# Low-rank weight tiles: loads moved to SyncE's queue, eight ahead, with six output buffers

## The chip, the cores and the metric

One core of one Trainium2 chip runs the kernel. The metric is the device time of one execution in microseconds (us). Engines are named as in the profile: PE is TensorE, DVE is VectorE, ACT is ScalarE, POOL is GpSimd, SP is SyncE, which here only issues transfers. SPq and ACTq are the instruction streams that issue transfers; a transfer's issue takes the issuing engine's time, its data lands later.

## The reference

Two attention-like and two feed-forward layers on x of 1024 rows by 512, each as `x = x + layernorm(layer(layernorm(x)))`. What matters here is the first layer and the weights of the last:

```
# layer 1: causal attention, 32 query heads of 16, 8 key/value groups, 4 heads each
q = x @ Wq ; kv = x @ Wkv ; softmax(q k^T / 4, causal) @ v ; @ Wo + bo
# layer 4: feed-forward whose three matrices have a low-rank part (rank 16)
out = x @ w.T + (x @ a.T) @ b.T          # gate, up: 1376 x 512; down: 512 x 1376
```

## The kernel before

The kernel folds the low-rank part of layer 4 into its weights: `w + b a` is computed once, tile by tile, and stored to DRAM (`lora_d`, `lorad_d`), from where it is read much later. There are 38 such tiles, `lora_jobs`: 0 to 10 of gate and 11 to 21 of up, 128 x 512 in float32 (the last of each has 96 rows), and 22 to 37 of down, 128 x 344. They are computed in the kernel's opening, in the gaps of the attention's projections and first scores.

One tile k takes five steps on four engines. PE multiplies `lora_bt` by `lora_at` (`lora_job`, L1078) into a PSUM bank; ACT copies it into an output buffer (`lora_take`, L899); POOL adds the weight tile that was loaded from DRAM (`pool_lora`, L1020); ACT issues the store (`lora_store`, L888) and, right behind it, the load of weight tile k + 4 into the buffer just read (`lora_load`, L882). ACT issues the store of tile k only after it took tile k + 2. Both rings have 4 buffers of 2 KiB per partition, so `lora_take` of tile k waits until the store of tile k - 4 has landed:

```
act.wait_ge(lora_ready, k + 1)
if k >= 4:
    act.wait_ge(lora_stored[k % 4], 16 * (k // 4))
```

The two operands: `lora_bt` is made by a DMA transpose (L398), `lora_at` by six copies from SBUF to SBUF (L400), all issued by SP once DVE has split the factors into bf16 pieces (`lora_split`).

Around this, the opening goes so. PE makes five projections of 16 float32 matmuls each (L1702): j = 0 the keys, j = 1 to 4 the queries, j = 1 holding those of groups 0 and 1. After each, ACT copies the PSUM banks to bf16 (L1669), DVE makes two further pieces (L1627 to L1631), SP stores the three (L1531) to `kp_d` or `qp_d`, and SP loads them back with another layout: the keys into `kt6` (L1535, six loads), a group's queries into `qt6` (`load_q`, L1253, six loads). SP's order is written by hand: stores of j = 0, loads of the keys, stores of j = 1, load of group 0's queries and a wait until it landed, stores of j = 2, 3, 4, three small loads (`sp_early`), load of group 1's queries, three hops.

With projection 4 PE begins the early scores (L1453): 80 score blocks, 48 of group 0 and 32 of group 1, of which eight lie in projection 4. DVE reduces each to row maxima (`row_max`, L1365 and L1369). When group 0 is through, `max_pieces` raises `m3_ready`, and SP sends the maxima by three hops (a DMA transpose L1260, a store L1263, a load L1266) into group 0's queries (`m_loaded`). Low-rank products 0 to 3, 4 to 7 and 8 to 11 are put between the matmuls of projections 2, 3 and 4 (`LORA_IN`), the other 26 (`LORA_LATE`) evenly between the 72 early scores that are left; PE waits with product k until product k - 4 was taken.

The group loop starts when all 38 tiles are taken (PE), the maxima of group 0 have landed, and all 38 stores have landed (ACT, `all_lora_stored`, since its output buffer overlaps theirs). Its eight groups follow one another, and then the feed-forward and the other layers.

Of the kernel before, what the change touches and what calls it, by code (L numbers as in the profile page):

```python
# [6 lines left out]
T, D = 1024, 512  # L7
NT, ND = T // P, D // P
# [70 lines left out]
def build(nc, x_in, Wq, Wkv, Wo, bo, gate_t, up_t, down_t, gate_s, up_s, down_s,  # L79
          gate_w, up_w, down_w, gate_a, gate_b, up_a, up_b, down_a, down_b, dft, power, inverse, out):  # L80
    with ExitStack() as ctx:
# [3 lines left out]
        def sem(name):  # L85
            return ctx.enter_context(nc.semaphore(name))
# [179 lines left out]
        lora_clear, lora_split, lora_stacked = sem("lora_clear"), sem("lora_split"), sem("lora_stacked")  # L266
        lora_w_loaded = [sem(f"lora_w_loaded{i}") for i in range(4)]
        lora_in, lora_ready, lora_taken = sem("lora_in"), sem("lora_ready"), sem("lora_taken")
        lora_stored = [sem(f"lora_stored{i}") for i in range(4)]
        prep_loaded = [sem(f"prep_loaded{b}") for b in range(4)]  # L270
# [55 lines left out]
        lora_bres = room(71.25, [NB, RANK])  # L326
        lora_out = room(176, [4, D])
        lora_w = room(152, [4, D])
        lora_jobs = [(m, n, 0) for m in range(2) for n in range(N1)] + [(2, n, j) for n in range(ND) for j in range(4)]
# [65 lines left out]
        def sp_lora_stack(sp):  # L395

            sp.wait_ge(lora_split, 1)
            sp.dma_start_transpose(lora_bt[:, :, :], lora_bs.rearrange("p n c -> p (n c)")).then_inc(lora_stacked, 16)  # L398
            for t, (_, piece) in enumerate(TERMS):
                sp.dma_start(lora_at[RANK * t:RANK * (t + 1), :], lora_ap[0:RANK, piece, :]).then_inc(lora_stacked, 16)  # L400
# [474 lines left out]
        def lora_bank(k):  # L875

            return 6 + k % 2 if k < LORA_LATE[0] else 4 + (k - LORA_LATE[0]) % 4

        def lora_load(act, k):

            src = lora_tile((gate_w, up_w, down_w), *lora_jobs[k])
            act.dma_start(lora_w[0:src.shape[0], k % 4, 0:src.shape[1]], src).then_inc(lora_w_loaded[k % 4], 16)  # L882

        def lora_store(act, k):

            act.wait_ge(lora_added, k + 1)
            dst = lora_tile((lora_d[0], lora_d[1], lorad_d), *lora_jobs[k])
            act.dma_start(dst, lora_out[0:dst.shape[0], k % 4, 0:dst.shape[1]]).then_inc(lora_stored[k % 4], 16)  # L888
            if k + 4 < len(lora_jobs):
                lora_load(act, k + 4)  # L890

        def lora_take(act, k):

            m, n, _ = lora_jobs[k]
            h, w = (height(m, n), D) if m < 2 else (P, FF1 // 4)
            act.wait_ge(lora_ready, k + 1)
            if k >= 4:
                act.wait_ge(lora_stored[k % 4], 16 * (k // 4))
            nc.scalar.copy(lora_out[0:h, k % 4, 0:w], ps[0:h, lora_bank(k), 0:w]).then_inc(lora_taken, 1)  # L899
            if k >= 2:  # L900
                lora_store(act, k - 2)


        LORA_IN = {j: range(4 * (j - 2), 4 * (j - 1)) for j in range(2, 1 + ND)}
        LORA_LATE = range(LORA_IN[ND][-1] + 1, len(lora_jobs))

        def all_lora_stored(engine):

            for k in range(4):
                engine.wait_ge(lora_stored[k], 16 * len(lora_jobs[k::4]))  # L910

# [102 lines left out]
        def pool_lora(pool):  # L1014

            for k, (m, n, j) in enumerate(lora_jobs):
                h, w = (height(m, n), D) if m < 2 else (P, FF1 // 4)
                pool.wait_ge(lora_taken, k + 1)
                pool.wait_ge(lora_w_loaded[k % 4], 16 * (k // 4 + 1))
                nc.gpsimd.tensor_tensor(lora_out[0:h, k % 4, 0:w], lora_out[0:h, k % 4, 0:w], lora_w[0:h, k % 4, 0:w],  # L1020
                                        ALU.add).then_inc(lora_added, 1)
# [492 lines left out]
        def _(sp):  # L1514
# [8 lines left out]
            sp.wait_ge(lora_clear, 1)  # L1523
            sp_lora(sp)
            sp_lora_stack(sp)

            for j in range(1 + ND):
# [9 lines left out]
                if j == 1:  # L1537
                    sp.wait_ge(pieces_stored[1], 48)
                    load_q(sp, 0)
                    sp.wait_ge(qt_loaded, 16 * len(TERMS))  # L1540
            sp.wait_ge(pieces_stored[0], 48 * 3)
            sp.wait_ge(pieces_stored[1], 48 * 2)
            sp_early(sp)
            load_q(sp, 1)
            for hop in range(3):
                maxima_hop(sp, 0, hop)

# [105 lines left out]
        def _(act):  # L1653
# [7 lines left out]
            for j in range(1 + ND):  # L1661
# [8 lines left out]
                if j == 0:  # L1670
                    act.wait_ge(v_psum, 1)
                    nc.scalar.copy(vall[:, :, :, :].rearrange("p t g d -> p (t g d)"),
                                   ps[:, 6:8, :].rearrange("p b n -> p (b n)")).then_inc(v_ready, 1)
                    for k in range(4):
                        lora_load(act, k)
            for k in LORA_LATE:
# [10 lines left out]
        def _(pe):  # L1687
# [36 lines left out]
            for j in range(1, 1 + ND):  # L1724
                if j >= 2:
                    pe.wait_ge(res_ready, j - 1)
                if j == 2:
                    pe.wait_ge(v_ready, 1)
                    pe.wait_ge(lora_stacked, 16 * 7)
# [89 lines left out]
```

## Time and profile before

| | |
|---|---|
| median of 3 runs | 921.38 us (920.71 to 922.01) |
| the profiled execution | 920.06 us, of it the span 918.0 us |
| busy in the span | PE 749.4 us, DVE 670.1, PEld 408.7, ACT 363.9, POOL 291.7 |
| PE clock granted, mean | 0.908 |
| DMA packets | 133360 on queue q1, 10816 on q10, 240 on q0 |
| low-rank stores issued by ACT to `lora_d` | 20 of 256 KB, median 4.5 us to landing |

Times are from the start of the span. A row of the timeline shows start, duration, engine, line, operation and, in brackets, the idle time before it and what ended it. Busy shares over the whole span say little of the opening, which is the first 150 us; it is read by stages. q1 is SP's queue and q10 is ACT's.

### The profile page before, as it was taken

How to read it: one execution, taken by the hardware profiler on the slowest of the kernel's cores; microseconds unless marked ns; L12 is line 12 of the kernel's file. 1: busy time of each engine (PE TensorE's matmuls, PEld its weight loads, DVE VectorE, ACT ScalarE, POOL GpSimd, SP SyncE). 2: the span in 40 equal slices, each digit the busy share in tenths (PEclk: the TensorE clock that was granted, in tenths of full speed). 3: DMA queues.
4: the chain of work that ended last, by engine and by line, in shares of the span. 5: the costliest groups of instructions: out<-in, count | busy, mean ns of one | idle time of the engine just before them, and what ended most of it. 6: DMA issues, size and time to landing. Idle time of an engine off the chain costs nothing. (4 is left out here: it accounts for less than half of the span.)

```text
span 918.0 us, 16061 instructions
## 1 busy us (share of the span) xinstructions
PE 749.4 (82%) x5081; PEld 408.7 (45%) x5102; DVE 670.1 (73%) x1781; ACT 363.9 (40%) x699; POOL 291.7 (32%) x348
## 2 busy tenths in 40 slices
PE   1967666879898898988869998696969999788694
PEld 1623221223222222222327676474747777566472
DVE  7523875766776767797489999896998999955713
ACT  1212224545565545677104444343433534323121
POOL 4024443102021120232104555345524335224131
PEclk9988656989899999998979999898989999899798
DMA  9499889772131312644451375613645221110100
GB/s 265 74 177 341 237 245 225 150 165 60 29 60 28 49 39 39 154 121 135 107 159 25 98 141 109 187 24 86 81 98 94 43 35 25 24 46 1 46 24 24
DMA packets 144477, 93.38 MB, mean 102 GB/s; under 512 B 111832, under 2 KB 123224, under 8 KB 144200
## 3 DMA queue, kind: packets, MB, share of 16 engines
q1 hardware_dynamic: 133360, 70.19, 34.4%
q10 hardware_dynamic: 10816, 16.91, 5.9%
q0 software_dynamic: 240, 5.51, 2.9%
q8 instruction: 33, 0.54, 0.3%
q14 instruction: 28, 0.23, 0.1%
HBM read 48.47 MB, written 29.04 MB: 84 GB/s over the span
## 5 line engine op out<-in xcount | busy, mean ns | idle before, releaser
L1205 PE MATMUL ps<-arena 128*128 128x256 f16 (+1 forms) x1952 | 238.2, 279 | 23.9 <-DMA arena<-arena 23.9
L1205 PEld LDWEIGHTS ps<-arena 128*128 128x128 f16 (+1 forms) x1952 | 196.4, 101 | 68.5 <-DMA arena<-arena 16.9
L1432 ACT ACTIVATE arena<-ps 128x1024 f32<-128x1024 f32 (+7 forms) x256 | 163.6, 651 | 123.4 <-PE ps L1462 118.8
L1453 PE MATMUL ps<-arena 96*128 (+4 forms) x384 | 137.0, 382 | 39.9 <-DVE mx L1369 15.5
L1365 DVE CUSTOM_DVE_ANT_0 arena<-ps,arena 128x256 bf16<-128x256 f32 (+3 forms) x256 | 122.0, 488 | 57.2 <-PE ps L1453 49.4
L1057 POOL TENSOR_TENSOR arena<-arena 128x256 f32<-128x256 f32 (+1 forms) x100 | 80.3, 803 | 258.3 <-ACT arena L948 257.6
L1227 PE MATMUL ps<-arena 128*128 128x512 f16 (+2 forms) x467 | 119.6, 385 | 32.6 <-POOL arena L1063 31.2
L1462 PE MATMUL ps<-arena 99*128 (+4 forms) x384 | 128.6, 352 | 4.6 <-ACT arena L1432 4.2
L1340 POOL TENSOR_SCALAR_AFFINE_SELECT arena<-arena 128x512 f32<-128x512 f32 x64 | 42.2, 659 | 230.4 <-ACT arena L1432 230.2
L1369 DVE TENSOR_REDUCE mx<-ps 128x1 f32<-128x512 f32 x128 | 88.2, 689 | 32.1 <-PE ps L1453 31.2
L1453 PEld LDWEIGHTS ps<-arena 96*128 (+1 forms) x384 | 39.3, 102 | 150.0 <-issue 81.0
L1485 PE MATMUL ps<-arena 128*32 128x256 f32 (+1 forms) x1280 | 100.7, 388 | 3.1 <-POOL arena L1340 2.3
L1227 PEld LDWEIGHTS ps<-arena 128*128 128x128 f16 (+1 forms) x488 | 46.1, 99 | 74.0 <-POOL arena L1063 36.6
L1063 POOL TENSOR_TENSOR arena<-arena 128x256 f16<-128x256 f32 (+1 forms) x100 | 77.6, 776 | 0.0
L1020 POOL TENSOR_TENSOR arena<-arena 128x512 f32<-128x512 f32 (+2 forms) x38 | 43.5, 1150 | 87.3 <-ACT arena L899 50.9
L947 ACT ACTIVATE arena<-ps,gs 128x256 f32<-128x256 f32 (+1 forms) x44 | 20.8, 473 | 122.4 <-PE ps L1205 122.4
L947 ACT ACTIVATE arena<-ps,sc 128x256 f32<-128x256 f32 x56 | 26.5, 474 | 85.3 <-PE ps L1205 85.3
L1462 PEld LDWEIGHTS ps<-arena 99*128 (+1 forms) x384 | 36.6, 100 | 41.2 <-issue 16.5
L1485 PEld LDWEIGHTS ps<-arena 128*32 128x32 f32 x1280 | 26.0, 110 | 53.4 <-issue 43.1
L1702 PE MATMUL ps<-arena 128*128 128x512 f32 x80 | 42.3, 660 | 6.8 <-DMA arena<-arena 6.0
L899 ACT COPY arena<-ps 128x512 f32<-128x512 f32 (+2 forms) x38 | 20.0, 526 | 66.0 <-DMA lora_d<-arena 28.1
L1183 PE MATMUL ps<-arena 128*128 128x256 f16 (+2 forms) x336 | 40.4, 280 | 7.0 <-DMA arena<-arena 6.3
(163 smaller groups left out, 851.9 us busy)
## 6 DMA issues: line engine op xcount, KB each, us to landing
arena<-qp_d SPq DMA_DIRECT2D x48, 128.0 KB, 4.1
lora_d<-arena ACTq DMA_DIRECT2D x20, 256.0 KB, 4.5
arena<-lora_d SPq DMA_DIRECT2D x10, 512.0 KB, 5.1
w1n_d<-arena SPq DMA_DIRECT2D x10, 512.0 KB, 3.6
arena<-rec_d SPq DMA_DIRECT2D x32, 128.0 KB, 2.6
qp_d<-arena SPq DMA_DIRECT2D x12, 256.0 KB, 4.9
w1dn_d<-arena SPq DMA_DIRECT2D x4, 704.0 KB, 3.8
arena<-in_L_ffn_down_w_dram ACTq DMA_DIRECT2D x16, 172.0 KB, 3.6
```

The source lines that it names most:

```text
L947: nc.scalar.activation(sg[0:h, b, :], ps[0:h, b, 0:CH], ACT.Silu, scale=gate[0:h, ht:ht + 1]).then_inc(sg_ready, 1)
L1020: nc.gpsimd.tensor_tensor(lora_out[0:h, k % 4, 0:w], lora_out[0:h, k % 4, 0:w], lora_w[0:h, k % 4, 0:w], ALU.add).then_inc(lora_added, 1)
L1057: nc.gpsimd.tensor_tensor(hs[0:h, b, :], sg[0:h, b, :], u_sb[0:h, b, :], ALU.mult).then_inc(hs_ready, 1)
L1063: nc.gpsimd.tensor_tensor(hid[0:h, 1, b, :], hs[0:h, b, :], hid[0:h, 0, b, :], ALU.subtract).then_inc(hid_ready, 1)
L1205: last = nc.tensor.matmul(ps[0:h, b, CH * o:CH * (o + 1)], w(t[0])[:, kt, ht * P:ht * P + h], xt[:, c, t[1], kt, :], start=(kt, t) == (0, ...
L1227: last = nc.tensor.matmul(ps[:, y_bank(k, i), :], hid[0:h, t[0], b, i * P:(i + 1) * P], down[0:h, ht, :], start=ht == 0 and t == terms[0], ...
L1365: nc.vector.tensor_tensor_reduce(out=junk[:, h, 0:w], in0=s_bank(g, u)[:, 0:w], in1=strip[:, D - w:D], scale=1.0, scalar=3.0 * NEG, op0=AL ...
L1369: nc.vector.reduce_max(mx[:, h, qt:qt + 1], s_bank(g, u)[:, 0:w], mybir.AxisListType.X).then_inc(s_taken, 1)
L1432: nc.scalar.activation(probs[:, kt % 2, h, kt * P:T], st_bank(h).rearrange("p b n -> p (b n)")[:, kt * P:T], ACT.Exp, scale=HD ** -0.5).th ...
L1453: nc.tensor.matmul(s_bank(g, u)[:, 0:k1 - k0], qt6[0:QROWS, g % RING, h, qt * P:(qt + 1) * P], kt6[0:QROWS, g, k0:k1], start=True, stop=Tr ...
L1462: last = nc.tensor.matmul(st_bank(h)[:, b, q0 - b * 512:512], kt6[0:QROWS + MROWS, g, kt * P:(kt + 1) * P], qt6[0:QROWS + MROWS, g % RING, ...
L1485: last = nc.tensor.matmul(o_bank[32 * h:32 * h + 32, b, q0 - b * 512:q1 - b * 512], vcur[:, kt, :], probs[:, kt % 2, h, q0:q1], start=kt = ...
```

## The change

The loads of the weight tiles go from ACT to SP, in a ring of 8 buffers: the first eight at the start, once the buffers' bytes are free (`xnt_psum`), 8 to 11 behind the piece stores of j = 3, 12 to 23 behind those of j = 4, and the rest between and behind the maxima's hops; load k waits until tile k - 8 was added. The output ring gets 6 buffers. The DMA transpose of `lora_bt` goes from SP to ACT. The products start one projection later: 0 to 3 in j = 3, 4 to 7 in j = 4, 30 late ones; with them moves PE's wait for the operands. The load of group 1's queries goes ahead of the stores of j = 2, and `sp_early` behind all loads.

```diff
@@ -264,9 +264,9 @@
         w0_loaded = [sem(f"w0_loaded{i}") for i in range(3)]
         lora_added = sem("lora_added")
         lora_clear, lora_split, lora_stacked = sem("lora_clear"), sem("lora_split"), sem("lora_stacked")
-        lora_w_loaded = [sem(f"lora_w_loaded{i}") for i in range(4)]
+        lora_w_loaded = [sem(f"lora_w_loaded{i}") for i in range(8)]
         lora_in, lora_ready, lora_taken = sem("lora_in"), sem("lora_ready"), sem("lora_taken")
-        lora_stored = [sem(f"lora_stored{i}") for i in range(4)]
+        lora_stored = [sem(f"lora_stored{i}") for i in range(6)]
         prep_loaded = [sem(f"prep_loaded{b}") for b in range(4)]
         prep_done = sem("prep_done")
         prep_stored = [sem(f"prep_stored{b}") for b in range(4)]
@@ -324,8 +324,10 @@
         lora_bt = room(63, [NB, P], BF16)
         lora_b = room(69.5, [NB, RANK])
         lora_bres = room(71.25, [NB, RANK])
-        lora_out = room(176, [4, D])
-        lora_w = room(152, [4, D])
+        LORA_DEEP = 8
+        LORA_OUT = 6
+        lora_out = room(176, [LORA_OUT, D])
+        lora_w = room(152, [LORA_DEEP, D])
         lora_jobs = [(m, n, 0) for m in range(2) for n in range(N1)] + [(2, n, j) for n in range(ND) for j in range(4)]
 
 
@@ -395,7 +397,6 @@
         def sp_lora_stack(sp):
 
             sp.wait_ge(lora_split, 1)
-            sp.dma_start_transpose(lora_bt[:, :, :], lora_bs.rearrange("p n c -> p (n c)")).then_inc(lora_stacked, 16)
             for t, (_, piece) in enumerate(TERMS):
                 sp.dma_start(lora_at[RANK * t:RANK * (t + 1), :], lora_ap[0:RANK, piece, :]).then_inc(lora_stacked, 16)
 
@@ -876,38 +877,44 @@
 
             return 6 + k % 2 if k < LORA_LATE[0] else 4 + (k - LORA_LATE[0]) % 4
 
-        def lora_load(act, k):
-
-            src = lora_tile((gate_w, up_w, down_w), *lora_jobs[k])
-            act.dma_start(lora_w[0:src.shape[0], k % 4, 0:src.shape[1]], src).then_inc(lora_w_loaded[k % 4], 16)
+        def lora_transpose(act):
+
+            act.wait_ge(lora_split, 1)
+            act.dma_start_transpose(lora_bt[:, :, :], lora_bs.rearrange("p n c -> p (n c)")).then_inc(lora_stacked, 16)
+
+        def lora_loads(sp, jobs):
+
+            for k in jobs:
+                if k >= LORA_DEEP:
+                    sp.wait_ge(lora_added, k - LORA_DEEP + 1)
+                src = lora_tile((gate_w, up_w, down_w), *lora_jobs[k])
+                sp.dma_start(lora_w[0:src.shape[0], k % LORA_DEEP, 0:src.shape[1]], src).then_inc(lora_w_loaded[k % LORA_DEEP], 16)
 
         def lora_store(act, k):
 
             act.wait_ge(lora_added, k + 1)
             dst = lora_tile((lora_d[0], lora_d[1], lorad_d), *lora_jobs[k])
-            act.dma_start(dst, lora_out[0:dst.shape[0], k % 4, 0:dst.shape[1]]).then_inc(lora_stored[k % 4], 16)
-            if k + 4 < len(lora_jobs):
-                lora_load(act, k + 4)
+            act.dma_start(dst, lora_out[0:dst.shape[0], k % LORA_OUT, 0:dst.shape[1]]).then_inc(lora_stored[k % LORA_OUT], 16)
 
         def lora_take(act, k):
 
             m, n, _ = lora_jobs[k]
             h, w = (height(m, n), D) if m < 2 else (P, FF1 // 4)
             act.wait_ge(lora_ready, k + 1)
-            if k >= 4:
-                act.wait_ge(lora_stored[k % 4], 16 * (k // 4))
-            nc.scalar.copy(lora_out[0:h, k % 4, 0:w], ps[0:h, lora_bank(k), 0:w]).then_inc(lora_taken, 1)
+            if k >= LORA_OUT:
+                act.wait_ge(lora_stored[k % LORA_OUT], 16 * (k // LORA_OUT))
+            nc.scalar.copy(lora_out[0:h, k % LORA_OUT, 0:w], ps[0:h, lora_bank(k), 0:w]).then_inc(lora_taken, 1)
             if k >= 2:
                 lora_store(act, k - 2)
 
 
-        LORA_IN = {j: range(4 * (j - 2), 4 * (j - 1)) for j in range(2, 1 + ND)}
+        LORA_IN = {j: range(4 * (j - 3), 4 * (j - 2)) for j in range(3, 1 + ND)}
         LORA_LATE = range(LORA_IN[ND][-1] + 1, len(lora_jobs))
 
         def all_lora_stored(engine):
 
-            for k in range(4):
-                engine.wait_ge(lora_stored[k], 16 * len(lora_jobs[k::4]))
+            for k in range(LORA_OUT):
+                engine.wait_ge(lora_stored[k], 16 * len(lora_jobs[k::LORA_OUT]))
 
 
         def down_read(engine, n):
@@ -1016,8 +1023,8 @@
             for k, (m, n, j) in enumerate(lora_jobs):
                 h, w = (height(m, n), D) if m < 2 else (P, FF1 // 4)
                 pool.wait_ge(lora_taken, k + 1)
-                pool.wait_ge(lora_w_loaded[k % 4], 16 * (k // 4 + 1))
-                nc.gpsimd.tensor_tensor(lora_out[0:h, k % 4, 0:w], lora_out[0:h, k % 4, 0:w], lora_w[0:h, k % 4, 0:w],
+                pool.wait_ge(lora_w_loaded[k % LORA_DEEP], 16 * (k // LORA_DEEP + 1))
+                nc.gpsimd.tensor_tensor(lora_out[0:h, k % LORA_OUT, 0:w], lora_out[0:h, k % LORA_OUT, 0:w], lora_w[0:h, k % LORA_DEEP, 0:w],
                                         ALU.add).then_inc(lora_added, 1)
 
         def pool_rest(pool):
@@ -1522,6 +1529,8 @@
                              Wo[half, :].rearrange("(c p) n -> p c n", p=P // 2)).then_inc(wo_loaded, 16)
             sp.wait_ge(lora_clear, 1)
             sp_lora(sp)
+            sp.wait_ge(xnt_psum, NT)
+            lora_loads(sp, range(LORA_DEEP))
             sp_lora_stack(sp)
 
             for j in range(1 + ND):
@@ -1538,12 +1547,19 @@
                     sp.wait_ge(pieces_stored[1], 48)
                     load_q(sp, 0)
                     sp.wait_ge(qt_loaded, 16 * len(TERMS))
+                    load_q(sp, 1)
+                if j == 3:
+                    lora_loads(sp, range(8, 12))
             sp.wait_ge(pieces_stored[0], 48 * 3)
             sp.wait_ge(pieces_stored[1], 48 * 2)
+            lora_loads(sp, range(12, 24))
+            maxima_hop(sp, 0, 0)
+            lora_loads(sp, range(24, 28))
+            maxima_hop(sp, 0, 1)
+            lora_loads(sp, range(28, 32))
+            maxima_hop(sp, 0, 2)
+            lora_loads(sp, range(32, len(lora_jobs)))
             sp_early(sp)
-            load_q(sp, 1)
-            for hop in range(3):
-                maxima_hop(sp, 0, hop)
 
             sp_group(sp, 0, 0, 0, 0)
             sp_tables(sp)
@@ -1671,8 +1687,7 @@
                     act.wait_ge(v_psum, 1)
                     nc.scalar.copy(vall[:, :, :, :].rearrange("p t g d -> p (t g d)"),
                                    ps[:, 6:8, :].rearrange("p b n -> p (b n)")).then_inc(v_ready, 1)
-                    for k in range(4):
-                        lora_load(act, k)
+                    lora_transpose(act)
             for k in LORA_LATE:
                 lora_take(act, k)
             for k in range(len(lora_jobs) - 2, len(lora_jobs)):
@@ -1724,7 +1739,7 @@
             for j in range(1, 1 + ND):
                 if j >= 2:
                     pe.wait_ge(res_ready, j - 1)
-                if j == 2:
+                if j == 3:
                     pe.wait_ge(v_ready, 1)
                     pe.wait_ge(lora_stacked, 16 * 7)
                 if j == ND:
```

The instruction order of SP in the opening, before. The rows from the copies of the low-rank operand to the last piece stores (L400 the copies, L1531 stores, L1535 the keys' loads, L1253 a group's queries):

```order
L398 DMA_TRANSPOSE arena<-arena 128x26x128
L400 DMA arena<-arena 16x2400 x6
L1531 DMA kp_d<-arena 128x1024 x3
L1535 DMA arena<-kp_d 16x8x1024 x6
L1531 DMA qp_d<-arena 128x1024 x3
L1253 DMA arena<-qp_d 16x4x1024 x6
L1531 DMA qp_d<-arena 128x1024 x9
```

The same place of SP's stream in the changed kernel (L891 is a weight tile's load, L401 the copies, L1540 stores, L1544 the keys' loads, L1260 the queries'):

```order
L891 DMA arena<-in_L_ffn_gate_w_dram 128x512 x8
L401 DMA arena<-arena 16x2400 x6
L1540 DMA kp_d<-arena 128x1024 x3
L1544 DMA arena<-kp_d 16x8x1024 x6
L1540 DMA qp_d<-arena 128x1024 x3
L1260 DMA arena<-qp_d 16x4x1024 x12
L1540 DMA qp_d<-arena 128x1024 x6
L891 DMA arena<-in_L_ffn_gate_w_dram 128x512 x2
L891 DMA arena<-in_L_ffn_gate_w_dram 96x512
L891 DMA arena<-in_L_ffn_up_w_dram 128x512
L1540 DMA qp_d<-arena 128x1024 x3
```

The transpose is gone from SP, eight loads stand ahead of the copies, and twelve query loads stand together, six of them ahead of the stores of j = 2. Further on in SP's stream, around the hops of the maxima (in this kernel L1267, L1270 and L1273), the changed kernel has:

```order
L891 DMA arena<-in_L_ffn_up_w_dram 96x512
L891 DMA arena<-in_L_ffn_down_w_dram 128x344 x2
L1267 DMA_TRANSPOSE mt<-m 128x128
L891 DMA arena<-in_L_ffn_down_w_dram 128x344 x4
L1270 DMA mt_d<-mt 128x128
L891 DMA arena<-in_L_ffn_down_w_dram 128x344 x4
L1273 DMA arena<-mt_d 3x4096
L891 DMA arena<-in_L_ffn_down_w_dram 128x344 x6
L377 DMA sc<-in_L_ffn_gate_s_dram 128x14x1
L378 DMA sc<-in_L_ffn_up_s_dram 128x14x1
L379 DMA row_b<-in_L_attn_bo_dram 128x512
```

Before, the three hops stood next to each other with nothing between. On PE, the start of the projections before (L1692 transposes, L1702 projections, L1720 the values, L1078 low-rank products):

```order
L1692 MATMUL ps<-ident,arena 128x128 x32
L1702 MATMUL ps<-arena 128x512 x8
L1720 MATMUL ps<-arena 128x128 x32
L1702 MATMUL ps<-arena 128x512 x9
L1078 MATMUL ps<-arena 128x512
L1702 MATMUL ps<-arena 128x512
```

and in the changed kernel (L1707, L1717, L1735 and L1085 are the same four):

```order
L1707 MATMUL ps<-ident,arena 128x128 x32
L1717 MATMUL ps<-arena 128x512 x8
L1735 MATMUL ps<-arena 128x128 x32
L1717 MATMUL ps<-arena 128x512 x17
L1085 MATMUL ps<-arena 128x512
L1717 MATMUL ps<-arena 128x512
```

Sixteen projection matmuls go through where eight did, before the first product and its wait.

## Rows read from the trace of the kernel before

**Rows 1.** Stages of the opening: length, busy (count) per engine, PEclk, DMA share, GB/s.

```profile
27.00:40.00 13.00, 13.00 (x71) 9.17 (x72) 10.13 (x11) 1.01 (x1) 0.00 (x0) 1.00 0.09 16
...
41.00:54.10 13.10, 7.08 (x18) 2.91 (x18) 5.35 (x6) 2.03 (x2) 0.00 (x0) 0.94 1.03 214
54.10:72.80 18.70, 14.56 (x31) 5.96 (x31) 3.14 (x3) 3.94 (x6) 5.35 (x5) 0.86 0.97 197
72.80:82.60 9.80, 8.01 (x13) 3.15 (x12) 0.92 (x1) 3.35 (x5) 4.71 (x4) 0.65 1.03 287
82.60:96.40 13.80, 9.47 (x31) 3.82 (x31) 10.67 (x19) 3.56 (x6) 6.50 (x5) 1.00 0.77 278
96.40:110.00 13.60, 11.99 (x36) 3.86 (x36) 12.75 (x52) 3.34 (x7) 8.38 (x7) 0.64 0.95 284
110.00:123.80 13.80, 7.02 (x19) 1.95 (x18) 8.00 (x24) 3.05 (x6) 5.83 (x6) 0.50 0.88 256
123.80:142.70 18.90, 11.85 (x38) 4.05 (x38) 14.04 (x56) 4.45 (x10) 9.07 (x10) 0.50 0.87 231
```

**Rows 2.** Timeline, 40 to 55 us: the low-rank operands and projection 2.

```profile
40.18 3.98 SPq L398 DMA_TRANSPOSE arena<-arena  x1
...
41.26 3.60 ACTq L882 DMA_DIRECT2D arena<-in_L_ffn_gate_w_dram  x4
...
44.21 4.01 SPq L400 DMA_DIRECT2D arena<-arena  x6
...
48.27 3.12 SPq L1531 DMA_DIRECT2D kp_d<-arena  x3
...
54.12 2.04 PE L1702 MATMUL ps<-arena 128*128 128x512 f32 x2 [6.04 <-DMA arena<-arena]
```

**Rows 3.** Timeline, 58 to 93 us: query stores, loads, first scores.

```profile
58.30 1.42 SPq L1531 DMA_DIRECT2D qp_d<-arena  x3
...
61.05 4.46 PE L1702 MATMUL ps<-arena 128*128 128x512 f32 x10
...
72.83 2.78 SPq L1253 DMA_DIRECT2D arena<-qp_d  x6
...
74.29 7.17 PE L1702 MATMUL ps<-arena 128*128 128x512 f32 x10
...
82.64 0.39 PE L1453 MATMUL ps<-arena 96*128 96x512 bf16 x1 [0.96 <-DMA arena<-qp_d]
...
92.22 1.01 ACT L1669 CAST arena<-ps 128x1024 bf16<-128x1024 f32 x1 [3.51 <-PE ps L1702]
```

**Rows 4.** Query loads of two later groups (L1253, 185 to 240 us): time to landing.

```profile
DMA to landing us min/median/max: 2.9/3.7/4.7
```

**Rows 5.** Waits, 96.4 to 150.2 us: total, times, longest.

```profile
ACT arena L899 <- DMA lora_d<-arena: 18.6, 9, 4.1
ACT arena L899 <- DMA lorad_d<-arena: 14.2, 10, 3.7
```

**Rows 6.** Groups of POOL, 96.4 to 148.2 us: busy, mean ns, idle before.

```profile
L1020 POOL TENSOR_TENSOR arena<-arena 128x344 f32<-128x344 f32 x16 | 14.5, 907 | 12.5 <-DMA arena<-in_L_ffn_down_w_dram 9.6 <-ACT arena L899 2.7
L1020 POOL TENSOR_TENSOR arena<-arena 128x512 f32<-128x512 f32 x9 | 11.7, 1307 | 16.5 <-DMA arena<-in_L_ffn_up_w_dram 10.6 <-ACT arena L899 5.9
```

**Rows 7.** Low-rank stores (L888, 96 to 150 us): time to landing.

```profile
DMA to landing us min/median/max: 1.8/3.2/8.6
```

**Rows 8.** Weight tiles' loads (L882, 96 to 150 us): time to landing.

```profile
DMA to landing us min/median/max: 2.6/4.0/9.3
```

**Rows 9.** The first hop's transpose (L1260, 100 to 180 us): time to landing.

```profile
DMA to landing us min/median/max: 3.8/5.9/8.1
```

**Rows 10.** Timeline, 123 to 151 us: first hop, end of the opening.

```profile
123.85 1.15 SPq L1260 DMA_TRANSPOSE mt<-m  x1
...
146.97 0.61 PE L1453 MATMUL ps<-arena 96*128 96x512 bf16 x1 [4.90 <-ACT arena L899]
...
150.14 1.94 ACT L1432 ACTIVATE arena<-ps 128x1024 f32<-128x1024 f32 x2 [3.22 <-DMA lorad_d<-arena]
```

## The prediction

> **What bounds it now.** I read the opening by stages first, since the change touches nothing behind it. In the stages [rows 1] the reader is to see that until 96.4 us no compute engine is full, while the DMA share is about 1.0 from 41 to 82.6 us; and that it was 0.09 from 27 to 40 us. Then the timeline [rows 2, 3] tells which transfer is waited for. Projection 2 starts at 54.12 after 6.04 us of waiting for a DMA: the copies of the low-rank operand, issued from 44.21, behind a transpose that held SP from 40.18. The same SP then stores the keys (48.27), and a strict chain follows, each link waiting for the landing of the one before: keys stored, keys loaded, queries of j = 1 stored (58.30), queries of group 0 loaded (72.83), first score (82.64). So the front is a chain of transfers, not PE.
>
> From 96.4 us on DVE could set the pace: it is busy 12.75 of 13.6 us, then 8.00 of 13.8 (to the first hop at 123.85 [rows 10]), then 14.04 of 18.9 [rows 1]. The 10 to 11 us that it lacks behind 110 us come from the low-rank ring: ACT waits 18.6 + 14.2 us for landed stores before it may take a tile [rows 5], PE waits for ACT and the scores stand behind PE's products. The end is the ring's too: PE starts the loop at 146.97 after 4.90 us of waiting for ACT, and the first exponential, at 150.14, waits for the last store [rows 10]. That start, 150.14, is the event I move. What follows is a loop whose transfers and casts are issued relative to it, so I carry a shift through to the end at full value; an earlier start has the same cold PE clock (0.50 [rows 1]) as now.
>
> **Part by part.**
>
> *Eight loads at 28 us, transpose to ACT.* The eight loads are 2 MB in a stretch where the DMA engines did 16 GB/s [rows 1], and the four that ACT issued at 41.26 [rows 2] are gone from the crowded one. At the issue times of that row (3.60 us for 4) eight take about 7 us, over by 35, before SP's next wait ends at 40.18. ACT issues the transpose at 41.3, free until its copy of 48.1, so it costs ACT nothing. SP's copies go out at 40.18 instead of 44.21 and the keys' stores at 44.2 instead of 48.27: minus 4.0. Bounds: minus 2 if transpose, copies and stores now share engines and land later, minus 4.1 by issue. PE's wait of 6.04 us leaves the front of projection 2; I count nothing for it, because PE then only comes sooner to the wait for group 0's queries.
>
> *Keys to group 0's queries.* 72.83 minus 58.30 is 14.5 us, mostly the keys' slow loads; four low-rank stores still fall beside them. I leave this link unchanged (bounds minus 2, plus 2). The next link took 9.8 us (72.83 to 82.64) beside the stores and loads of some four low-rank tiles on ACT's queue (POOL's four adds in that stage [rows 1]). Now no low-rank load stands there. Six issues take 2.78 us [rows 3] and a quiet landing 3.7 (at most 4.7) [rows 4]: 6.5 us, minus 3.3. Upper bound 9.8 as before. First score: 82.6 - 4.0 - 3.3 = 75.3.
>
> *Projection 4.* PE now is at its wait from about 64 us (projections 2 and 3 from 48 us on, 7.1 us each at the 4.46 us for ten matmuls of [rows 3], and four products with ACT's takes) and stands 11 us, so its clock will have fallen. The price is in two rows of equal work: ten projection matmuls took 4.46 us at 61.05 and 7.17 at 74.29 [rows 3]: 2.7 us. Against it stand 1.5 us, since DVE has finished the pieces of j = 3 by then and PE needn't wait for it as it did now and then before. The projection took 9.6 us (82.64 to 92.22) [rows 3]; it will take 10.8 and end at 86.1. Group 1's queries and the stores of j = 2, which ACT's copy needs, are issued from 75.3 to 80 and should land by 85. Shift at the end of the pieces (96.4 before): minus 6.1.
>
> *Late scores up to the first hop.* DVE's work there is 12.75 + 8.00, 20.8 us [rows 1], in 27.4 us. With six buffers the ring is no more the brake: take k + 6 needs store k, issued behind take k + 2, so four tiles turn in about 0.6 + 0.3 + 3.2 + 0.6, 4.7 us [rows 7], 1.2 us a tile; by the longer landing of 8.6 it would be 2.5, as slow as now. POOL needs 1.31 us a tile of 512 and 0.91 of 344 [rows 6], which is now the ring's pace. Tile 12's load stands behind the landing of the last piece stores and costs POOL a gap of 2 to 3 us, which the ten tiles of slack in banks and buffers mostly absorb. I add 1.7 us of stall: 22.5 us instead of 27.4, minus 4.9. Bounds: minus 6.6 (none), 0 (landings as long as their longest). First hop at 112.8.
>
> *From the first hop to the loop.* SP issues loads 24 to 27 only when the maxima are ready, 28 to 31 only when the transpose has landed, 32 to 37 only when the store behind it has. This is the wait that the change adds, and behind it stand POOL, ACT, PE. With the transpose at 5.9 us [rows 9], a store at 3.2 and a tile load at 4.0 [rows 8], and about 1.5 us of issues between, loads 32 on land 14.6 us after the hop; six more adds are 5.4 us, the last store 3.2: 23.2 us. The scores alone want DVE 14.04 us, so they don't decide. Before it was 150.14 - 123.85, 26.3 us: minus 3.1. With the shortest landings (3.8, 1.8, 2.6, the last store 1.8) it is 16.9 us, minus 9.4; with the longest (8.1, 8.6, 9.3, the last store as above) 36.1, plus 9.8.
>
> *Nothing for the rest.* `sp_early` and group 2's queries now come at 127 to 132 us, ahead of the loop's start; their cover is its first part. Were it gone, each would cost its landing, 4 us.
>
> Sum: -4.0 - 3.3 + 1.2 (together minus 6.1), -4.9, -3.1: **minus 14.1 us**. First exponential at 136.0; the profiled execution 920.06 - 14.1 = 906.0, and 1.3 us more against the median shown, 921.38: **907.3 us**.
>
> **Weighed against the skill.** The late stages must move their 11.8 MB (rates by lengths in [rows 1]) in some 41 us instead of 46: 288 GB/s, just what the stages from 72.8 and 96.4 us reached, so there is room, but not much. The Trainium skill, "DMA: Bandwidth & Descriptors", section "Issuing engines are not separate DMA queues", says that transfers issued from SP and ACT run on the same 16 engines, so that spreading them saves issue time only. By it alone the ring's part of the gain would have to come from the buffers, or not at all, which is the first rival's time.
>
> **Rivals.**
> - *The DMA engines are the limit.* For it: share 0.87 to 0.95 behind 96.4 us [rows 1]. Against it: the bytes, and 0.09 ahead of 40 us, where 2 MB now go. The late stages then keep their 46 us and the front brings 6.1: 915.3.
> - *All landings short.* The front as forecast, 6.1, and the lower bounds of the two late stages, 6.6 and 9.4: minus 22.1, 899.3.
> - *The change does nothing:* if the loop start were held by something else. POOL's adds total only 26 us in 52 [rows 6], and nothing else waits at 146.97. 921.
> - *Slower: loads trapped between the hops.* One mechanism: the last 14 tiles wait for two landings of a three-link chain and then for their own. If the landings there are the longest seen, 36.1 us instead of 26.3, the loss is 9.8 there, less 6.1 in the front, and crowded engines that let landings grow so leave the scores' stage where it was: 925.1. It decides from 32.4 us on (26.3 + 6.1); with the scores' gain, from 37.3. The skill's page of the same title, section "Queues, rings and completion order", says that an engine takes from each queue in turn; by it the hops, now behind tile loads in SP's own queue, come later, and the stores, alone in ACT's, sooner. No row here shows the two apart.
>
> **Chances and range.** Forecast (902 to 911) 0.60; DMA limit 0.20; short landings 0.10; nothing 0.04; slower 0.06. What a measurement can tell from no change is 0.2%, 1.8 us. Faster 0.90, same 0.04, slower 0.06. The range takes in the forecast, most of the first rival and the near part of the second: 902 to 915.5.
>
> **What would show it.** In the new profile: eight gate loads by 35 us; no PE wait at projection 2, but one of about 11 us in projection 4; first score near 75, first hop near 113, with DVE over 90% busy between 90 and 113; POOL waiting for down tiles at two places behind the hop; first exponential near 136; from there on a copy of the old trace. It is wrong if the first score comes at 80 or later (the queries' landing), if ACT still waits over 20 us for stores, or if the time from the first hop to the loop grows beyond 28 us.

## The result, and the profile after

The changed kernel is slower: 925.31 us median (918.56 to 933.49, 20 runs) against 922.07 (916.25 to 930.42, 20 runs) before, ratio 1.0049, interval 1.0028 to 1.0071. The forecast was 907.3, faster. Its profiled execution took 928.51 us, span 926.4; before's 920.06, span 918.0.

The opening of the changed kernel by stages (columns as in [rows 1]; the second to last is the DMA share):

```profile
27.00:40.00 13.00, 13.00 (x76) 9.41 (x76) 9.61 (x11) 1.01 (x1) 0.00 (x0) 1.00 0.57 178
...
92.60:117.60 25.00, 18.86 (x57) 6.30 (x57) 22.46 (x74) 9.16 (x17) 18.80 (x16) 0.64 0.93 325
117.60:134.80 17.20, 12.18 (x39) 4.22 (x39) 13.90 (x56) 4.97 (x12) 10.74 (x13) 0.50 0.92 257
...
134.80:160.10 25.30, 4.02 (x9) 1.04 (x9) 3.42 (x7) 0.00 (x0) 2.61 (x4) 0.50 0.94 219
```

The eight loads fill the gap ahead of 40 us. Until 134.8 us things go as forecast, less well but in the same direction: DVE is busy 22.46 of 25.0 us up to the first hop. Then comes a stage that has no counterpart before: 25 us in which ACT does nothing and PE 4 us of work, with the DMA share at 0.94. The timeline of the changed kernel, with the events that answer to those of [rows 2], [rows 3] and [rows 10]:

```profile
40.71 7.11 SPq L401 DMA_DIRECT2D arena<-arena  x6
40.71 5.21 ACTq L883 DMA_TRANSPOSE arena<-arena  x1
...
47.86 2.59 SPq L1540 DMA_DIRECT2D kp_d<-arena  x3
...
70.65 10.36 SPq L1260 DMA_DIRECT2D arena<-qp_d  x12
...
78.38 0.61 PE L1460 MATMUL ps<-arena 96*128 96x512 bf16 x1 [8.01 <-DMA arena<-qp_d]
...
117.58 1.22 SPq L1267 DMA_TRANSPOSE mt<-m  x1
...
134.76 2.27 ACTq L897 DMA_DIRECT2D lorad_d<-arena  x3
134.85 0.61 PE L1460 MATMUL ps<-arena 96*128 96x512 bf16 x1 [3.17 <-ACT arena L906]
...
136.40 0.52 POOL L1607 DMA_DIRECT2D w0u_d<-in_L_ffn_up_t_dram  x1
136.91 0.50 POOL L1608 DMA_DIRECT2D w0d_d<-in_L_ffn_down_t_dram  x1
...
160.15 1.94 ACT L1439 ACTIVATE arena<-ps 128x1024 f32<-128x1024 f32 x2 [25.35 <-DMA lorad_d<-arena]
```

First score 4.3 us earlier than before (78.38 against 82.64), first hop 6.3 (117.58 against 123.85), PE's loop start 12.1 (134.85 against 146.97). Then ACT waits 25.35 us for the last stores, where it waited 3.22 [rows 10], and its first exponential is 10.0 us later than before. What stands beside those stores are the two casts that POOL issues right behind its last add (`up_t` and `down_t` to 16-bit copies in DRAM, each 1792 KB). The DMA view of 130 to 165 us, with packets, MB and share of 16 engines, and the issues with their median time to landing:

```profile
q0 software_dynamic: 160, 3.67, 48.7%
...
w0u_d<-in_L_ffn_up_t_dram POOLq DMA_DIRECT2D x1, 1792.0 KB, 14.4
w0d_d<-in_L_ffn_down_t_dram POOLq DMA_DIRECT2D x1, 1792.0 KB, 22.8
lorad_d<-arena ACTq DMA_DIRECT2D x7, 172.0 KB, 5.8
```

The landing of the last five stores (L897, 133 us on), against a longest of 8.6 before [rows 7]:

```profile
DMA to landing us min/median/max: 5.2/6.5/23.6
```

The packet records of the trace show the mechanism. The two casts travel in 128 packets of 28,672 bytes, 2.13 us each; a store's row is a packet of 1376 bytes, 0.07 us. From the records, the starts of packets in us from the span's start:

```
kernel, execution     first cast packet   last cast packet   last store packet   store packets behind the first cast packet
before                149.77              167.71             149.76              0
before, once more     148.61              166.60             148.65              3
changed               140.22              157.53             159.99              249
changed, once more    138.53              156.04             158.32              200
```

From 142.2 to 157.5 us 111 cast packets began and 120 store packets: about one small packet goes for each long one. So 249 small packets, 0.07 us of an engine's time each, last until the casts are through. In the kernel before, the last store packet began 7 ns ahead of the first cast packet; in its second profile three began behind it. By the Trainium skill, "DMA: Bandwidth & Descriptors", section "Queues, rings and completion order", each engine takes from the queues in turn, a packet at a time; the trace agrees, with 111 packets of 2.13 us beside 120 of 0.07. The forecast cited that section for the hops, and not for this.

### The profile page after: what moved, and what is told of

Read it like the earlier page. It is cut to its first block and busy times, and to the rows that moved or that the text cites. A ratio compares the mean times of both kernels' runs of the same rounds, so it can differ in the third digit from the quotient of the medians.

```text
span 926.4 us, 16081 instructions
## 1 busy us (share of the span) xinstructions
PE 749.2 (81%) x5102; PEld 407.6 (44%) x5102; DVE 674.2 (73%) x1781; ACT 363.5 (39%) x699; POOL 290.8 (31%) x348
## 5 line engine op out<-in xcount | busy, mean ns | idle before, releaser
L1234 PE MATMUL ps<-arena 128*128 128x512 f16 (+2 forms) x488 | 124.5, 386 | 29.2 <-POOL arena L1070 29.1
L954 ACT ACTIVATE arena<-ps,gs 128x256 f32<-128x256 f32 (+1 forms) x44 | 20.8, 473 | 122.7 <-PE ps L1212 122.7
L1717 PE MATMUL ps<-arena 128*128 128x512 f32 x80 | 38.8, 620 | 6.7 <-DMA arena<-kp_d 5.8
L963 ACT CAST arena<-arena 128x256 f16<-128x256 f32 (+1 forms) x100 | 40.3, 403 | 1.8 <-POOL arena L1064 1.8
```

The source lines that it names most:

```text
L954: nc.scalar.activation(sg[0:h, b, :], ps[0:h, b, 0:CH], ACT.Silu, scale=gate[0:h, ht:ht + 1]).then_inc(sg_ready, 1)
L1234: last = nc.tensor.matmul(ps[:, y_bank(k, i), :], hid[0:h, t[0], b, i * P:(i + 1) * P], down[0:h, ht, :], start=ht == 0 and t == terms[0], ...
```

## The experiments

Ten edited kernels ran, and the two kernels once more. Ratios are to the kernel before on the same chip, with their interval.

**e1_casts_wait.**

```diff
             pool_lora(pool)
+            all_lora_stored(pool)
             pool.dma_start(w16_d[1], up_t).then_inc(w0_cast[1], 16)
```

> The changed kernel, with GpSimd waiting for the landing of all low-rank stores before it issues the two casts. Theory (the last stores are starved behind the casts' 28,672-byte packets, 2.1 us each): the first exponential, at 160.15 us in the changed kernel, comes at about 141, 4 to 6 us behind the last store's issue; about 907 to 910 us, ratio to before near 0.985. Rival (the stores are held by the 4-byte packets and query loads of SyncE's own queue, or by the stores themselves): the exponential stays near 160 and the time near 925.

Measured: 911.87 us, ratio 0.9914 (0.9884 to 0.9944). The last store packet is at 142.93, the first cast packet at 145.30, and the timeline has

```profile
143.27 1.94 ACT L1439 ACTIVATE arena<-ps 128x1024 f32<-128x1024 f32 x2 [8.02 <-DMA lorad_d<-arena]
```

The casts made the stall: without them beside the stores the exponential comes 17 us sooner. It is 2 us later than expected, and ACT's wait is still 8.02 us. SP's small loads and query loads are issued in the same moment as the last stores, which here land up to 6.9 us after their issue; in f1 below, where the small loads are gone from this place and the queries are earlier, it is at most 4.0.

**e2_act_late_wait.**

```diff
-            all_lora_stored(act)
-            for_groups(act, act_group)
+            act_group(act, 0, 0)
+            all_lora_stored(act)
+            ...
```

> The changed kernel, with ScalarE's wait for the landed stores moved behind its group 0; the casts stay where they are. Theory (everything queued is starved while the casts run): the first exponential comes right behind the first scores, near 136.5, but TensorE then waits for group 2's queries, whose load has a landing of up to 19 us, until 150 or so; about 910 to 914 us. Rival (only ScalarE's wait matters): no such second wait, about 903 us.

Measured: 914.8 us, ratio 0.9923 (0.9885 to 0.9962). The exponentials start at 136.54, and the stall comes back at the next thing that was queued, group 2's queries, issued from 133.3 with a landing of up to 22.7 us:

```profile
158.47 0.61 PE L1460 MATMUL ps<-arena 96*128 96x512 bf16 x1 [10.78 <-DMA arena<-qp_d]
```

So it isn't ACT's wait alone: a load on SP's queue is held as the stores on ACT's are. The rival is out. PE's wait ends at 158.5, later than the 150 expected.

**e3_small_loads_first.**

```diff
+            sp_early(sp)
             lora_loads(sp, range(12, 24))
...
             lora_loads(sp, range(32, len(lora_jobs)))
-            sp_early(sp)
```

> The changed kernel, with the three small loads (two scale vectors in 4-byte pieces, one bias row) ahead of tile load 12 instead of behind the last tile load. Theory with the small loads as what makes the last stores late for the casts: few or no store packets are left when the first cast packet starts, first exponential at 139 to 142, about 908 us, perhaps not in every execution. If they don't matter: 925 us, and still some 249 store packets behind the first cast packet.

Measured: 909.27 us, ratio 0.9897 (0.9851 to 0.9943). 3 store packets were behind the first cast packet (142.58 against 142.54), and

```profile
139.86 0.61 PE L1460 MATMUL ps<-arena 96*128 96x512 bf16 x1 [5.28 <-ACT arena L906]
...
143.02 1.94 ACT L1439 ACTIVATE arena<-ps 128x1024 f32<-128x1024 f32 x2 [3.21 <-DMA lorad_d<-arena]
```

With the casts left where they are the race is won again, but not because the last stores end much sooner: their last packet begins at 142.58 here and at 142.93 in e1. What changed is its distance from the last add, 1.8 us here (the add ends at 140.79), 6.3 in e1 (136.65); POOL issues the casts right behind that add. The price is that the adds end 4.3 us later than in the changed kernel (136.46) and the loop starts 5 us later on PE, since the small loads now stand ahead of the tile loads. So two 7 KB loads in 4-byte pieces and a bias row, moved behind the tile loads at no cost by the forecast, made the last stores late for the casts. Whether by their own packets or by the query loads that they push beside the last stores is not separated: here, and in f1, both are out of the way.

**e4_before_casts_wait.** The same line as in e1, in the kernel before.

> The kernel before, with GpSimd waiting for all stores before the casts. In its profiled execution the last store packet ended 7 ns ahead of the first cast packet, so nothing was starved. Theory: same within 0.3%, or a little faster and with less spread, if other executions lose that race. Rival (the later casts cost something further on): slower by up to 2 us.

Measured: 921.96 us, ratio 1.002 (0.9983 to 1.0057): no difference that the interval of some 0.4% either way can tell. Nothing shows that before loses to the casts, or that later casts cost anything.

**c1_before_casts_early.** Both casts of the kernel before, issued four adds sooner:

```diff
             for k, (m, n, j) in enumerate(lora_jobs):
+                if k == len(lora_jobs) - 4:
+                    pool.dma_start(w16_d[1], up_t).then_inc(w0_cast[1], 16)
+                    pool.dma_start(w16_d[2], down_t).then_inc(w0_cast[2], 16)
...
             pool_lora(pool)
-            pool.dma_start(w16_d[1], up_t).then_inc(w0_cast[1], 16)
-            pool.dma_start(w16_d[2], down_t).then_inc(w0_cast[2], 16)
```

> The kernel before, with GpSimd issuing the two casts four adds earlier (behind the add of tile 33, not 37), so that they start some 6 us sooner and meet the last loads and stores. Theory (whatever is queued when the casts start is starved until they end, some 18 us later): first exponential at 160 to 166 us instead of 150, about 932 to 936 us, ratio 1.012 to 1.016. Rival (the stall in the changed kernel came from something the change added on SyncE's queue): 922 us, no slower.

Measured: 934.09 us, ratio 1.0117 (1.0073 to 1.0161). 890 store packets stood behind the first cast packet (143.88). From 145.9 to 161.2 us, with no query load beside them, 111 cast packets began and 112 store packets. And

```profile
165.29 0.61 PE L1456 MATMUL ps<-arena 96*128 96x512 bf16 x1 [23.78 <-ACT arena L899]
```

The stall can be made in the kernel before, with nothing of the change in it. The first exponential, at 168.17, is later than expected and 18.0 us later than before; the span is only 14.6 longer (932.6). A part of a late start is given back further on, which the forecast had excluded.

**f1_all_apart.** The edits of e1 and e2, and:

```diff
             lora_loads(sp, range(32, len(lora_jobs)))
-            sp_early(sp)
 
             sp_group(sp, 0, 0, 0, 0)
+            sp_early(sp)
             sp_tables(sp)
```

> The changed kernel with three edits: the casts wait for all stores, ScalarE waits for them behind its group 0 only, and the three small loads go behind group 1's hops, ahead of the tables. Nothing that the loop's start needs is then behind the casts or the 4-byte packets. Theory: loop start on TensorE at 134 to 135, first exponential at 136 to 137, no wait for group 2's queries, ratio 0.983 to 0.986 (about 905 to 907 us where before has 920), which is the size forecast for the change. If the opening's gain does not carry through: no better than e1 and e3 (0.990).

Measured: 915.09 us, ratio 0.9918 (0.9883 to 0.9952); the expectation failed. The exponentials start at 139.4, earlier than in e1 or e3, but the span is 920.5 in this execution, 781 us behind that start where before has 768 (918.0 - 150.14). This profiled execution was the slowest of the ten (922.56), so some 7 of these 13 us are its own and not the kernel's. The waits of 160 to 225 us name a place for the rest:

```profile
PE ps L1460 <- DMA arena<-qp_d: 12.6, 1, 12.6
```

It is group 1, where PE waits for group 3's queries. SP issues those behind group 1's hops, the gate weights' transpose, (here) the small loads, the tables and the up weights' transpose. In e1, whose exponentials start 3.9 us later, it is 5.8 us. The kernel before has the same wait, in rows that the forecast did not look at. Its waits and SP's timeline:

```profile
PE ps L1453 <- DMA arena<-qp_d: 5.1, 1, 5.1
```

```profile
162.38 4.78 SPq L1260 DMA_TRANSPOSE mt<-m  x1
170.45 0.36 SPq L1263 DMA_DIRECT2D mt_d<-mt  x1
171.94 0.27 SPq L1266 DMA_DIRECT2D arena<-mt_d  x1
172.67 8.31 SPq L411 DMA_TRANSPOSE arena<-w0g_d  x1
...
184.12 8.23 SPq L411 DMA_TRANSPOSE arena<-w0u_d  x1
192.90 4.06 SPq L1253 DMA_DIRECT2D arena<-qp_d  x6
```

The hop at 162.38 needs 8 us until 170.45; the last cast packet ends at 169.7. In the changed kernel the stall lets the casts end first:

```profile
172.81 1.11 SPq L1267 DMA_TRANSPOSE mt<-m  x1
175.07 0.37 SPq L1270 DMA_DIRECT2D mt_d<-mt  x1
```

That hop takes 2.3 us, and the wait for the queries is gone.

**h0_before_w0u_later.** This tests the reading on the kernel before:

```diff
             all_lora_stored(sp)
-            sp_weights0(sp, 1)
-            with sp.Fori(1, ND + 1) as g:
+            sp_group(sp, 1, 1, 0, 1)
+            with sp.Fori(2, ND + 1) as g:
```

> The kernel before, with SyncE's DMA transpose of the up weights (8 us of issue) moved from ahead of group 3's query load to behind group 1's other transfers. In before's group 1 TensorE waits 5.1 us for those queries, which in the changed kernel it doesn't. Theory (that wait is what the stalled start pays back in the changed kernel): group 1 takes 38 to 39 us instead of 42.9 between its first exponentials, ratio 0.994 to 0.997. Rival (group 1's length has another cause): 42 us or more, ratio 1.0.

Measured: 920.22 us, ratio 0.9962 (0.9931 to 0.9993). No DMA wait is left in group 1, and it takes 38.5 us where before's, the second row, takes 42.9 (stages as above):

```profile
189.80:228.30 38.50, 33.90 (x257) 10.73 (x256) 27.39 (x87) 21.37 (x34) 7.63 (x10) 0.96 0.41 72
```

```profile
185.30:228.20 42.90, 35.11 (x257) 11.17 (x256) 27.55 (x87) 21.38 (x34) 7.63 (x10) 0.90 0.47 105
```

Of these 4.4 us 1.2 are PE's busy time, at a granted clock of 0.96 against 0.90, and 3.2 its idle time. By the ratio the edit is worth 0.4%, 3.5 us, as expected. The span, 916.8, shows little of it, because in this execution the opening ran later (first exponential at 154.48, for a reason not looked into).

**u1_four_buffers.** e1 with `LORA_OUT = 4`.

> e1_casts_wait with four output buffers instead of six. If the output ring set the pace of the late scores (a step of the forecast): ScalarE waits for landed stores again for 20 us or more, first exponential 5 to 8 us later than in e1 (148 to 151), ratio 0.996 to 1.0. If the loads eight ahead did it: as e1, 0.991.

Measured: 918.69 us, ratio 0.996 (0.9938 to 0.9982). First exponential at 151.41, 8.1 us later than in e1. Its waits of 88 to 150 us:

```profile
ACT arena L906 <- DMA lora_d<-arena: 20.1, 14, 4.3
ACT arena L906 <- DMA lorad_d<-arena: 16.6, 9, 4.0
```

These are 36.7 us, like the 32.8 of [rows 5]; in e1 they are 9.0. The six buffers are what opened the late stretch.

**u2_products_from_2.** e1 with `LORA_IN` and PE's wait as before, at projection 2.

> e1_casts_wait with the products from projection 2 on, as before. If the later start matters: TensorE waits at projection 2 for the operands, the queries' stores meet more traffic, first score 1 to 3 us later than 78. If it doesn't (the chain of transfers sets the first score): first score within 1 us, and four tiles fewer in the late stretch; time within 0.2% of e1.

Measured: 917.43 us, ratio 0.9968 (0.9933 to 1.0003). First score at 79.08, about as in e1. But the first exponential is at 147.9, 4.6 us later than in e1, for a reason that neither side had named:

```profile
POOL arena L1027 <- DMA arena<-in_L_ffn_gate_w_dram: 17.5, 1, 17.5
```

Twelve products are in flight before projection 4 is done, but tile 8's load stands in SP's order behind the piece stores of j = 3. The later start of the products fits the place of the loads; in the front it saves nothing (the first score is at 79.06 in e1).

**h1_best.** e1's and e3's edits, and h0's.

> The changed kernel with the casts behind all stores, the three small loads ahead of tile load 12, and the up weights' transpose behind group 1. First exponential at 141 to 144 us, no wait for group 3's queries, group 1 at 38 to 39 us; ratio 0.984 to 0.988. If the two repairs don't add up, 0.990 as e3.

Measured: 908.98 us, ratio 0.9861 (0.9825 to 0.9896), faster than both kernels. First exponential at 143.29, no DMA wait in group 1. Its interval overlaps e3's (0.9851 to 0.9943), so the ratios alone don't show that h0's edit adds to e3's.

**after_again** and **before_again.** Both kernels once more, for a second profile.

> The changed kernel once more, for its profile alone. If the stall at the casts is in every execution: first exponential at 158 to 162 us again, with over 100 store packets behind the first cast packet, and no DMA wait in group 1. If it is a matter of luck: 139 to 145.

> The kernel before once more, for its profile alone. Its profiled execution won the race of the last store against the first cast by 7 ns. If that is typical: first exponential at 149 to 151 us. If other executions lose it: up to 168.

Measured: changed 925.9 us (span 923.8), before 919.63 (span 917.6). The first exponentials are at 158.48 and 149.00, and the changed kernel has

```profile
ACT arena L1439 <- DMA lorad_d<-arena: 24.9, 1, 24.9
```

so the stall is in both of its profiled executions, and in neither of before's.

## Why the prediction was wrong

**The step that failed** is "six more adds are 5.4 us, the last store 3.2: 23.2 us", in the part from the first hop to the loop. The adds were right: POOL's last one ended at 136.46, 18.9 us behind the hop where the sum has 20.0, and POOL issued the casts there. The last store took 23.6 us and not 3.2, and the stretch from hop to first exponential 42.6 us (160.15 - 117.58) instead of 23.2. The landing was priced from stores that had no cast beside them. With the casts held back, in e1, it is at most 6.9 us: the casts made 16.7 of the 20.4 us that were missed, and what SP issues in that moment probably most of the rest (in f1, without it, at most 4.0). That POOL issues two casts right behind its last add was in the source and in before's timeline (at 147.93 us), and the forecast never asked what the last stores would share the engines with. e1 and c1 show the cause from both sides, e2 that it holds SP's queue as well as ACT's. Two of the forecast's own signs of being wrong came true here: ACT waited over 20 us for stores, and the last stretch grew beyond 28 us. Added up against before, the three parts brought -3.8, -2.4 and +16.3 us, where -6.1, -4.9 and -3.1 were forecast.

**Nothing for `sp_early`** was wrong too, and it is the change's own part in the stall. The forecast asked who waits for these loads, and not whom they delay. In the changed kernel the small loads and group 2's queries are issued from 127.8 to 136.6 us, when the last stores are; e3 shows that with the loads elsewhere only 3 packets are behind the cast, at the price of later adds.

**The front** was forecast at minus 6.1 us and brought 3.8 (the last pieces end at 92.6 against 96.4). The term of 4.0 for the keys' stores came out as 0.4: the six copies, issued while the transpose ran on ACT, took 7.11 us of issue instead of 4.01 [rows 2], so that the term fell short even of its lower bound, 2. It is so in all nine profiles that have the transpose on ACT (6.1 to 7.3 us, against 3.8 to 4.0 in the five that have it on SP), but since no run leaves the transpose out, it is not shown to be the cause. The keys and the stores of j = 1 gained 1.8 (47.86 to 70.65 against 48.27 to 72.83), and group 0's queries 2.1 instead of 3.3.

**The late scores** took 25.0 us up to the first hop instead of 22.5 (27.4 before): half the forecast gain. The step on the ring was right: in u1 four buffers cost 8.1 us, 3.0 of them ahead of the first hop. DVE stood 2.5 us, not 1.7; the larger error is in its work, 22.46 us where the sum has 20.8. Two small operations on the maxima grew, here in the kernel before, then in the changed one:

```profile
122.46 0.41 DVE L1377 TENSOR_TENSOR mx<-mx 128x16 f32<-128x16 f32 x1
122.90 0.18 DVE L1382 TENSOR_SCALAR m<-mx 128x32 bf16<-128x32 f32 x1
```

```profile
111.34 5.43 POOL L1027 TENSOR_TENSOR arena<-arena 128x512 f32<-128x512 f32 x5
114.24 1.70 DVE L1384 TENSOR_TENSOR mx<-mx 128x16 f32<-128x16 f32 x1
115.98 0.83 DVE L1389 TENSOR_SCALAR m<-mx 128x32 bf16<-128x32 f32 x1
116.85 0.19 DVE L1390 SCALAR_TENSOR_TENSOR mr<-mx,m 128x32 f32<-128x32 f32 x1
```

They lie beside adds of POOL that follow one another without a gap until 116.77, and the next operation is quick again. Six more profiles with such adds beside them show the same (e1 with 1.95 and 0.84 us, for one). In u2 POOL's adds pause from 121.14 to 127.10 us, and the same two, at 121.97, take 0.17 and 0.18. So DVE's times were taken from a stage in which POOL's adds had gaps, and the change closed the gaps. No experiment was made for this alone.

**Carried "through to the end at full value"** was wrong by a few microseconds, in the changed kernel's favour. Behind the first exponential, before needs 767.9 and 768.6 us, the changed kernel 766.3 and 765.3. Group 1 takes 42.9 us before and 38.3 in the changed kernel's first profile, with no wait for the queries, which is what h0 takes away. But the clock weighs as much: in its second profile the group takes 42.2 with no DMA wait, at a granted clock of 0.84 (0.90 before, 0.96 in h0):

```profile
193.80:236.00 42.20, 38.02 (x257) 11.36 (x256) 27.43 (x87) 21.40 (x34) 7.64 (x10) 0.84 0.32 62
```

**A reading.** That until 96.4 us no compute engine is full is wrong for 27 to 40 us, where PE is busy 13.00 of 13.00 us [rows 1]; no term rests on it.

**The rivals.** "The DMA engines are the limit" had the late stages keep their 46 us. They took 42.2 (92.6 to 134.8), and the one ahead of the first hop moved 325 GB/s where 284 and 256 were moved before, so a share near 0.9 was not the end of what the engines give. The slower rival, loads trapped between the hops, cost POOL one wait of 4.92 us and decided nothing: from the first hop to PE's loop start are 17.3 us, 23.1 before. Its time, 925.1, is the one that was measured (925.31), but by chance: the loss came from a mechanism that no rival named.

**What stays open.** The profiled spans of the changed kernel are 7.3 us longer on average (926.4 and 923.8 against 918.0 and 917.6), the medians of 20 runs only 3.2 us. Single executions of both kernels spread over some 14 us, and only profiled ones show their stages. Whether some of the changed kernel's executions escape the stall was not shown, nor how much of the late landings in e1 is due to the 4-byte pieces and how much to the query loads.

## What to carry to other kernels

When a stage is made to end sooner, ask what is issued at its end and with what size of packet: a bulk transfer from another queue that used to start just behind the last small stores may now start ahead of them, and hold them for its whole length, as it did here. Let a bulk transfer that nobody needs yet wait for the landing of what the next stage does need (here one wait, worth 1.3% between the changed kernel's 1.0049 and e1's 0.9914). A transfer that is "hidden" must be priced twice: by who waits for it and by whom it keeps waiting.

## What the runs showed of the hardware that was not expected

- A cast from DRAM to DRAM on POOL's queue went out as packets of 28,672 bytes, 2.13 us each. Beside them, store packets of 1376 bytes on ACT's queue began about one for one (120 beside 111, in c1 112 beside 111), so that the last of 249 began at 159.99, and query loads on SP's queue took up to 22.7 us to land (e2).
- Loads in 4-byte pieces, 9 ns a piece, kept the engines busy for long: from 131 to 135 us SP's queue passed 600 to 1200 of them per microsecond, for 14 KB in all, with the DMA share (of all queues) at 1.18 to 1.22.
- SP's issue of six copies took 7.11 us while ACT's queue ran a DMA transpose, and 4.01 behind one on its own queue [rows 2]. The cause was not isolated.
- Two small DVE operations beside gapless POOL adds took 1.70 and 0.83 us, and 0.17 and 0.18 in u2, where POOL paused. No experiment was made for this alone.
